# Order of the first loads and of TensorE's first products in a fused attention and expert block

## The reference

```python
# cond: quantised weight plus a low-rank delta
lora_delta = lora_B @ lora_A * (32 / 64)
normalized = (weight + lora_delta) / scale                  # groups of 128 inputs
w_eff = cb[searchsorted(thresholds, normalized)] * scale + lora_delta
c = x @ w_eff.T
# attention with one head of d = 128
q, k, v = split(c @ Wqkv + bqkv)
x = x + (softmax(q @ k.T / sqrt(d)) @ v) @ Wo + bo
# cond2: base product plus top-2 of 8 low-rank experts
base = x @ W.T
gates = top-2 softmax of (x @ Wr.T + 5 * one_hot(language))
m = base + 2 * sum over experts of gate * (x @ A_e.T) @ B_e.T
# ffn: dequantised weight
x = x + m @ (scale * (qweight - zero_point)).T + bias
```

## Time and profile before

| what | value |
|---|---|
| median of three executions | 108.63 us (107.9, 108.68, 108.63) |
| the profiled execution's own time | 108.59 us |
| its span | 106.6 us |
| PE busy, 513 products | 102.3 us (96% of the span) |
| DVE busy | 68.7 us (65%) |
| ACT busy | 52.1 us (49%) |
| POOL busy | 31.7 us (30%) |
| PEclk, the granted TensorE clock, in tenths | 9 (full) in each of 40 slices |

### The profile page before, as it was taken

The page is one execution under the profiler, slowest core; times in us unless marked ns, Lnnn a source line. Parts: engine busy times, 40 slices in busy tenths (PEclk is TensorE's granted clock), DMA queues, the critical chain, the costliest instruction groups (busy, mean ns, idle before and its releaser), DMA issues.

```text
span 106.6 us, 1460 instructions
## 1 busy us (share of the span) xinstructions
PE 102.3 (96%) x513; PEld 84.6 (79%) x513; DVE 68.7 (65%) x164; ACT 52.1 (49%) x92; POOL 31.7 (30%) x40
## 2 busy tenths in 40 slices
PE   6999999999999999999999999999999999999980
PEld 6747758889788889899888786888899888888850
DVE  4358799979999999814999853004946802482441
ACT  4038989999989960845122239272028104002000
POOL 4000045799907590199100037400000400000000
PEclk9999999999999999999999999999999999999999
DMA  1798999980000000000000000000000550000072
GB/s 45 204 312 268 412 399 405 406 318 6 0 3 0 0 0 0 3 6 0 0 0 0 0 0 0 6 0 0 0 0 0 208 185 0 6 0 0 3 295 98
DMA packets 4471, 9.57 MB, mean 90 GB/s; under 512 B 752, under 2 KB 1008, under 8 KB 4464
## 3 DMA queue, kind: packets, MB, share of 16 engines
q1 hardware_dynamic: 4384, 9.35, 24.5%
q10 hardware_dynamic: 80, 0.13, 0.4%
HBM read 7.38 MB, written 2.10 MB: 89 GB/s over the span
## 4 chain that ended last, share of the span: by engine, by line
PE 92%; DVE 2%; ACT 1%; DVEq 1%; issue 0%
PE psum L861 19%; PE psum L863 19%; PE psum L862 19%; PE psum L887 7%; PE psum L878 5%; PE psum L869 4%; PE psum L897 3%; PE psum L912 3%; PE psum L903 3%; PE psum L907 3%; PE psum L1012 2%; PE psum L1033 2%; PE psum L1027 2%; ACT moe L462 1%; PE psum L1019 1%; PE psum L928 1%
## 5 line engine op out<-in xcount | busy, mean ns | idle before, releaser
L663 DVE COPY_PREDICATED cond_work<-cond_work,psum 128x1024 f32<-128x1024 int32 x10 | 13.7, 1368 | 1.2 <-ACT cond_work L363 0.8
L861 PE MATMUL psum<-G_hi,xT_hi 128*128 128x512 f32 x32 | 12.7, 398 | 0.0
L863 PE MATMUL psum<-G_hi,xT_lo 128*128 128x512 f32 x32 | 12.5, 390 | 0.0
L862 PE MATMUL psum<-G_lo,xT_hi 128*128 128x512 f32 x32 | 12.5, 390 | 0.0
L363 ACT ACTIVATE cond_work<-cond_n,cut_bias 128x1024 f32<-128x1024 f32 x10 | 11.3, 1145 | 0.6 <-DVE cond_n L700 0.6
L578 POOL TENSOR_TENSOR hl<-hl,hl_bias 128x272 f32<-128x272 f32 (+2 forms) x4 | 3.1, 772 | 26.3 <-ACT hl L374 14.4
L523 POOL TENSOR_TENSOR xT_lo<-xT,xT_hi 128x1024 fp32r<-128x1024 f32 x4 | 9.6, 2405 | 3.2 <-DVE cond_work L669 3.2
L861 PE MATMUL psum<-xT_hi,split_b_hi 128*128 128x512 f32 x24 | 9.7, 402 | 0.0
L863 PE MATMUL psum<-xT_hi,split_b_lo 128*128 128x512 f32 x24 | 9.4, 392 | 0.0
L862 PE MATMUL psum<-xT_lo,split_b_hi 128*128 128x512 f32 x24 | 9.4, 390 | 0.0
L887 PE MATMUL psum<-hlT,xT 128*128 128x136 f32 x64 | 8.3, 280 | 0.0
(11 more groups left out here) (167 smaller groups left out, 240.3 us busy)
## 6 DMA issues: line engine op xcount, KB each, us to landing
out<-cond_work SPq DMA_DIRECT2D x7, 256.0 KB, 2.1
cond_n<-in_cond_w SPq DMA_DIRECT2D x2, 512.0 KB, 6.8
xT<-in_x_t SPq DMA_DIRECT2D x2, 512.0 KB, 7.9
q_i<-in_q_t SPq DMA_DIRECT2D x4, 256.0 KB, 7.5
moe<-in_moe_w SPq DMA_DIRECT2D x4, 256.0 KB, 7.7
xT<-in_x_t SPq DMA_DIRECT2D x1, 1024.0 KB, 12.7
wqkv_n<-in_wqkv SPq DMA_DIRECT2D x1, 768.0 KB, 10.6
hlT<-in_hl_t SPq DMA_DIRECT2D x1, 272.0 KB, 6.0
```

What stands on the lines that cost most here:

```text
L663: dve.copy_predicated(half(level, h), beyond[n % len(beyond)].bitcast(I32), psum[EARLY][:, j + 1:j + 2].to_broadcast([P, 2 * C])).then_inc ...
L861: pe.matmul(out_ap, l_hi, r_hi, start=first, stop=False)
L862: pe.matmul(out_ap, l_hi, r_lo, start=False, stop=False)
L863: return pe.matmul(out_ap, l_lo, r_hi, start=False, stop=last)
```

## The change

- The warm-up becomes 2 products of 128 x 512 (before: 7 of 128 x 128), so `blank` is 128 x 512. The four products behind delta are dropped.
- TensorE runs G_first before x_hl(0).
- SyncE loads q0 and moe0 ahead of cond_w0, and cond_w1 behind moe3.
- VectorE runs w_full(0) before w_delta_first.
- The remainders of w_eff tiles 0 and 1 move from VectorE to GpSimd (`w_eff_rest`), each ahead of the wqkv remainder of the same number. Tiles 2 and 3 stay on VectorE with a semaphore of their own.

```diff
--- before.py
+++ after.py
@@ -64,8 +64,7 @@
     LANG_BIAS = 5.0
     EXPERT_SCALE = 32.0 / 16.0
     CODEBOOK_FLOOR = 1e-8
-    WARM_UP = 7
-    FILL = 4
+    WARM_UP = 2
     X_LOADS = ("x0", "x0", "x1", "x1", "x2", "x2", "x2", "x2")
     HL_PARTS = ((0, 1), (2, 3), (4,), (5, 6, 7))
     assert SEQ == P and D == P and ER == P and HL == ER + E and HT == 512 and C == 512
@@ -96,7 +95,7 @@
 
         ident = sb("ident", [P, P])
         ident_r = sb("ident_r", [P, P], F32R)
-        blank = sb("blank", [P, P])
+        blank = sb("blank", [P, C])
         lora = sb("lora", [P, 2, C])
         hlT = sb("hlT", [P, CT, HL])
         xT = sb("xT", [P, PAIRS, CT, PT])
@@ -243,7 +242,7 @@
         inv_scale_ready = sem("inv_scale_ready")
         wd_ready = sem("wd_ready")
         w_eff_ready = sem("w_eff_ready")
-        w_eff_lo_ready = sem("w_eff_lo_ready")
+        w_eff_late_lo_ready = sem("w_eff_late_lo_ready")
         bo_G_ready = sem("bo_G_ready")
         bo_HL_ready = sem("bo_HL_ready")
         M_lo_ready = sem("M_lo_ready")
@@ -264,6 +263,7 @@
         y_bias_ready = sem("y_bias_ready")
         wd_late_ready = sem("wd_late_ready")
         norm_late_ready = sem("norm_late_ready")
+        w_eff_lo_ready = sem("w_eff_lo_ready")
         level_late_set = sem("level_late_set")
         moe_lo_ready = sem("moe_lo_ready")
         expb_lo_ready = sem("expb_lo_ready")
@@ -287,14 +287,14 @@
 
             load("lora_b", lora[0:RANK, 0, :], lora_in[0:RANK, 0, :])
             load("small", small[:, :], small_in)
+            load_proj_weights(0)
             load("cond_w0", cond_n[:, 0:2, :], cond_w[:, 0:2, :])
             load("hlT", hlT[:, :, :], hl_t)
             load("x0", xT[:, 0, :, :], x_t[0])
-            load_proj_weights(0)
             load_proj_weights(1)
-            load("cond_w1", cond_n[:, 2:4, :], cond_w[:, 2:4, :])
             load_proj_weights(2)
             load_proj_weights(3)
+            load("cond_w1", cond_n[:, 2:4, :], cond_w[:, 2:4, :])
             load("x1", xT[:, 1, :, :], x_t[1])
             load("woT", woT[:, :, :], wo_t)
             load("exp_b", expb[:, :, :], exp_b)
@@ -537,6 +537,10 @@
                 pool.wait_ge(wqkv_hi_ready, o + 1)
                 rest(wqkv_lo[:, o, :], wqkv_n[:, o, :], wqkv_hi[:, o, :], wqkv_ready)
 
+            def w_eff_rest(o):
+                pool.wait_ge(w_eff_hi_ready, o + 1)
+                rest(split_a_lo[:, o, :], level[:, o, :], split_a_hi[:, o, :], w_eff_lo_ready)
+
             def moe_rest(o):
                 pool.wait_ge(moe_hi_ready, o)
                 rest(split_a_lo[:, o, :], moe[:, o, :], split_a_hi[:, o, :], moe_lo_ready)
@@ -559,12 +563,13 @@
             x_lo(0)
             pool.wait_ge(w_eff_ready, 2)
             x_lo(1)
+            w_eff_rest(0)
             wqkv_rest(0)
-            pool.wait_ge(w_eff_lo_ready, 2)
+            w_eff_rest(1)
             wqkv_rest(1)
             wqkv_rest(2)
             wqkv_rest(3)
-            pool.wait_ge(w_eff_lo_ready, CT)
+            pool.wait_ge(w_eff_late_lo_ready, 2)
             pool.wait_ge(woT_hi_ready, 1)
             rest(woT_lo, woT[:, :, :], woT_hi, woT_lo_ready)
             x_lo(2)
@@ -673,7 +678,7 @@
             def w_eff_lo(o):
                 dve.wait_ge(w_eff_hi_ready, o + 1)
                 dve.tensor_tensor(split_a_lo[:, o, :], level[:, o, :], split_a_hi[:, o, :], ALU.subtract)\
-                   .then_inc(w_eff_lo_ready, 1)
+                   .then_inc(w_eff_late_lo_ready, 1)
 
             def G_rest(i):
                 dve.wait_ge(G_hi_ready, i + 1)
@@ -694,12 +699,12 @@
             alone(dve.tensor_tensor(cuts[:, 2:3], cuts[:, 2:3], cuts[:, 3:4], ALU.min))
             dve.tensor_scalar(cut_bias[:, :], cuts[:, :], -CUT_GAIN, None, ALU.mult).then_inc(cut_bias_ready, 1)
 
+            w_full(0)
             w_delta_first()
             dve.wait_ge(wd_ready, 1)
             dve.wait_ge(inv_scale_ready, 1)
             dve.tensor_tensor(blocks(0), blocks(0), inv_scale[:, 0:GROUPS // 2].unsqueeze(2).to_broadcast(
                 [P, GROUPS // 2, P]), ALU.mult).then_inc(norm_first_ready, 1)
-            w_full(0)
             pick(0, 0)
             w_full(1)
             pick(1, 0)
@@ -724,8 +729,6 @@
                .then_inc(Bf_lo_ready, 1)
             pick(2, 1)
             pick(3, 1)
-            w_eff_lo(0)
-            w_eff_lo(1)
             pick(4, 1)
             pick(5, 1)
             pick(6, 1)
@@ -864,12 +867,8 @@
 
 
             pe.wait_ge(blank_ready, 1)
-            def idle_turns(n):
-                for _ in range(n):
-                    pe.matmul(psum[6][:, 0:P], blank[:, :], blank[:, :], start=True, stop=True)
-
-            idle_turns(WARM_UP)
-
+            for _ in range(WARM_UP):
+                pe.matmul(psum[6][:, :], blank[:, 0:P], blank[:, :], start=True, stop=True)
 
             pe.wait_ge(loaded["lora_b"], 16)
             pe.wait_ge(loaded["lora_a"], 16)
@@ -877,7 +876,6 @@
             for o in range(CT):
                 pe.matmul(psum[o][:, :], lora[:, 0, o * P:(o + 1) * P], lora[:, 1, :], start=True, stop=True)\
                   .then_inc(delta_done, 1)
-            idle_turns(FILL)
 
             def x_hl(part, bank, batches=None, base=0):
                 for t in (batches or HL_PARTS[part]):
@@ -914,9 +912,9 @@
                         pe.matmul(psum[i][:, s], ident_r[:, :], ident_r[:, :], start=False, stop=True)\
                           .then_inc(G_done, 1)
 
+            G_first()
             pe.wait_ge(loaded["hlT"], 16)
             x_hl(0, 4)
-            G_first()
             G_product(1)
             G_product(2)
             pe.wait_ge(ident_r_ready, 1)
@@ -985,7 +983,7 @@
             pe.wait_ge(wqkv_ready, CT)
             for i in range(CT):
                 for o in range(2, CT):
-                    pe.wait_ge(w_eff_lo_ready, o + 1)
+                    pe.wait_ge(w_eff_late_lo_ready, o - 1)
                     mm = M_part(o, i)
                 mm.then_inc(M_done, 1)
```

## The result

The changed kernel takes 108.8 us in the median of 20 executions (108.54 to 109.98), the kernel before 108.34 us in 20 (107.82 to 108.68). The ratio is 1.006 with a 95% interval of 1.004 to 1.008: no change by the bound of 1%, but a small loss that is clear of the noise. The profiled execution of the changed kernel was the slowest of its 20, 109.98 us with a span of 107.9, so it shows the mechanism larger than the median has it. The ratios leave out executions that took over 1.5% more than the fastest of their kernel.

A forecast was written before the change was run, and what follows sets the result against it. TensorE was taken to bound the kernel; its earlier readiness is lost waiting for the later cond_w0 chain, so 108.59 + 0.07 = 108.66, forecast as 108.7 us, no change (0.78), range 107.7 to 109.6.

The forecast's parts named there:

- What bounds the kernel: Whole run: TensorE, busy 102.3 of 106.6 us; only less work on it or a faster rate shortens the run.
- Warm-up: Start of TensorE: starts at 1.37, new warm-up ends at 4.78; delta starts 0.38 us later and ends 0.2 late.
- The moment of the rise: During delta's products: TensorE's rate doubles at 7.1 us, assumed to stay there.
- Rival C: At delta: clock rises with the new warm-up; waits take all (108.7 us), otherwise 106.8; chance of over 1% gain 0.07.
- cond_w0's landing: Load ahead of w_delta_first: lands at 8.95 instead of 7.7 us, bounds 8.3 to 9.6, making the chain 0.65 later.
- Meeting point: At G_product(1): TensorE waits for w_hi(1), then w_lo(1); second four products start at 16.34, not 16.27, plus 0.07 us.
- Remainders on GpSimd: Two w_eff remainders moved from VectorE: GpSimd has slack of 0.9 and 0.7 us before TensorE's use, cost 0.
- Rival D: At VectorE's picks: GpSimd and VectorE block each other, two picks 1.29 us late each, 109.7 us; chance 0.03.
- Rival B: At w_delta_first: cond_w0 lands beyond 9.5, costing 1 us per us, 109.3 at 9.6, 109.9 at 10.2; chance 0.12.

The follow-up runs named there:

- e0: The changed kernel run and profiled again with no edit: median 109.27 us against 108.04 for the kernel before, ratio 1.0104.
- e2: The kernel before with only SyncE's load order changed (q0 and moe0 ahead of cond_w0, cond_w1 behind moe3): ratio 1.0126 to the kernel before.
- e5: The changed kernel with the old warm-up (seven products of 128 columns, small blank tile): ratio 1.0066 to the kernel before.
- e14: e13 with w_full(1) before pick(0, 0) and w_lo(1) before pick(1, 0) on VectorE: ratio 1.0113 to the kernel before.
- e4: The changed kernel with the remainders of w_eff tiles 0 and 1 back on VectorE: ratio 1.0071 to the kernel before.
- e9: The changed kernel with VectorE forming Bf_lo before w_eff(1): ratio 1.0102 to the kernel before.
- e1: The kernel before without the four idle products behind delta: ratio 0.9982 to the kernel before.
- e3: The changed kernel with the old load order, x_hl(0) ahead of G_first and w_full(0) behind the scaling: ratio 1.001 to the kernel before.
- e10: The kernel before without idle products behind delta, and with Bf_lo before w_eff(1) on VectorE: ratio 1.003 to the kernel before.
- e13: e10 with GpSimd forming wo's remainder before it waits for w_eff's last remainders: ratio 0.9993 to the kernel before.
- e6: The changed kernel with cond_w0 loaded behind hlT and x0 too: ratio 1.0372 to the kernel before, profiled 111.89 us.

## Why the prediction was right, and where not

The forecast was 108.7 us and no change by the bound of 1%; measured were 108.8 us and a ratio of 1.006. Part of the agreement is luck. The forecast added 0.07 us to 108.59 and 108.63, one profiled execution and the median of three; the median of 20 is 108.34, so the loss is 0.46 us by the medians and not 0.07, and 1.2 us in the repeat (e0). The class is right by the first set; in the repeat the middle of the ratio lies just beyond 1%.

- *What bounds the kernel, and that the chain from cond_w0 takes the place of TensorE's work*: right. The wait is at G_product(1) for w_hi(1), as forecast, and e2 to e5 put the cost on the order of the loads, and none on warm-up or remainders. That the load is cond_w0 rests on the column of constants, on e0 and on the waits for w_hi(1), not on e2.
- *Warm-up*: the start at 1.37 was 1.45. The first product behind delta came at 9.62 (line 895) and in the kernel before at 9.16 (an idle one), 0.46 us later where 0.2 was forecast. The moment of the rise, held for fixed at 7.1, is not fixed: by the weight loads it lay at about 7.4 in the changed kernel's profile, by 5.1 in e5's and before 4.4 in e14's, both with the old warm-up. Rival C's early rise so came without the large products, and with its forecast result: all of it was lost in waits. (Its place of 13.7 for TensorE should be 8.2 + 1.85 + 3.43 = 13.5; nothing hangs on it.)
- *cond_w0's landing*: forecast 8.95, within 8.3 to 9.6. Six profiles with this order had 8.34 (e4), 8.55 (e5), 9.01 (e0), 9.16 (e9), 9.40 (e2) and 9.80 (changed, the slowest of its 20 executions). The term was right in the middle, the bounds too narrow at the upper end. Its base of 7.7 is late for the old order: the other five profiles with it (e1, e3, e10, e13, e14) had 7.0 to 7.6.
- *Meeting point*: this is the step that failed, in the sentence that behind it "TensorE is not held again". Its price for a landing of 8.95 was plus 0.07 us. The two waits that it named came, and e0, with its add at 9.04, has 0.14 at this point. But the chain holds TensorE at y_x(0) too, through Bf_lo, with 0.33 us of slack before instead of 0.62, and each wait costs 0.11 us more at the product behind it. At y_x(0) e0 is 0.43 us late, and at its end 0.62 (109.21 against 108.59). I had compared only the rounds of G_product with TensorE's pace and not carried the 0.65 us down VectorE's list to its next customer. The forecast landed near the median because its base was too high by 0.3 us and because at the median the landing was earlier than 8.95: 108.8 less 100.15 stands for an add at 8.65. That last step is worked out from the profiles' constant, not seen in a profile of a median execution.
- *Remainders on GpSimd*: right, cost 0 (e4). But x_lo, which queues behind them, did not have "several us to spare": in the kernel before x_lo(3) ended 0.11 us ahead of the cast, and e10 ran into it. *Rival D* in the form given, picks held up, did not occur: picks ran beside GpSimd at 1.43 us each. The rule of the Trainium skill ("SBUF — State Buffer", "Who interferes with whom"), as the prediction gives it, has two SBUF inputs as its condition, and a pick reads one of its operands from psum, so the prediction had put it to the wrong instructions. That VectorE and GpSimd exclude each other for a whole instruction, when both want the ports that they share, is borne out by other rows: the cast ended 0.03 us after GpSimd in e10 and e9, and w_lo(1), with two SBUF inputs, took twice its time in e14. How complete the exclusion is stays open: blocked to the end of GpSimd's row, w_lo(1) and w_full(2) would have ended at 14.90 and 17.39, and they ended at 14.76 and 17.14.
- *Rival B*: e6 is its case. Its price of 1 us per us holds from an add at 8.36 to one at 9.83, with up to 1.27 us of idle time; at 10.65, with 2.0 us, the clock added 1.1 us of its own.

## What to carry to other kernels

When a chain feeds a busy engine, list every place at which that engine takes something from the chain and write the slack at each; the smallest slack is the gain that a change can keep, and a loss starts behind it. Take the base of the sum from many executions: here three gave 0.3 us too much. A load put forward puts others back: count the bytes ahead of each of them, and ask for each what starts with it. When an engine's list is full, look at its small items too, since a cast of 0.16 us can wait for another engine's 2.4 us instruction.

## What the runs showed that was not expected

- The granted clock on the page is full in the first slices, while weight loads last 0.33 us instead of 0.19 until the rise. The rise itself lay anywhere from before 4.4 us (e14) to 7.4 us (changed), and with the same seven products ahead of it from before 4.4 to 7.1 (kernel before).
- 2.0 us without a product were followed by a granted clock of 0.50 (e6). 1.27 us (e5) and 1.6 us (e2, e14) were not.
- The time of an execution follows from a single event, the start of VectorE's add, to within 0.02 us in five profiles, two of the changed kernel and three of its variants (e3, e4, e5).
- An int32 cast of 8 elements per partition lasted 0.83 us (e10) and 0.61 us (e9) in place of 0.16, until GpSimd was done.
